# A graph network kernel: six gathers in flight, indices a block ahead, ACT's order changed, source tables split in place

## The reference

```python
edge_in = concatenate([edges, nodes[receivers], nodes[senders]], axis=-1)
h = relu(edge_in @ We1 + be1)
new_edges = h @ We2 + be2
agg = segment_sum(new_edges, receivers, num_segments=nodes.shape[0])
```

## Time and profile before

| | us |
|---|---|
| runs, median of 3 | 4964.16 |
| lowest and highest run | 4954.04, 4967.15 |
| the profiled execution | 4958.28 |
| its span | 4956.7 |
| PE busy | 4118.4 (83%) |
| VectorE busy | 3063.9 (62%) |
| POOL busy | 2552.3 (51%) |
| ACT busy | 1450.4 (29%) |

### The profile page before, as it was taken

How to read it: one execution, slowest core, us unless ns; L and a number is a source line. 1 busy time by engine, 2 the same in 40 slices (tenths; PEclk the granted TensorE clock), 3 DMA queues, 4 the chain that set the end, 5 groups by cost and what they waited for, 6 DMA issues and landing times.

```text
span 4956.7 us, 144137 instructions
## 1 busy us (share of the span) xinstructions
PE 4118.4 (83%) x56332; PEld 3710.4 (75%) x56332; DVE 3063.9 (62%) x4215; ACT 1450.4 (29%) x2353; POOL 2552.3 (51%) x2291
## 2 busy tenths in 40 slices
PE   1777799987999981999999999899758989999596
PEld 0566688887999981777777777777548988888596
DVE  5999888881111023777777777777437777777612
ACT  0333599990000012222222222222222222222100
POOL 0388766665665676666666666666003433333200
PEclk9766899998999995999999999999859999999798
DMA  5510488889999955776676777677326766666496
GB/s 173 203 30 29 144 317 321 323 320 315 397 383 417 417 199 187 226 232 220 227 235 228 227 235 229 224 230 236 128 78 219 235 207 205 221 221 214 135 399 260
DMA packets 430602, 1170.77 MB, mean 236 GB/s; under 512 B 111223, under 2 KB 250470, under 8 KB 422760
## 3 DMA queue, kind: packets, MB, share of 16 engines
q1 hardware_dynamic: 331910, 929.09, 53.0%
q0 software_dynamic: 66016, 114.12, 7.9%
q10 hardware_dynamic: 32256, 121.34, 6.2%
HBM read 798.21 MB, written 368.14 MB: 235 GB/s over the span
## 4 chain that ended last, share of the span: by engine, by line
DMA 41%; issue 27%; POOL 16%; PE 9%; DVE 4%; POOLq 2%; SPq 1%; ACT 0%; ACTq 0%; DVEq 0%
DMA feat_slot<-SK,sidx_p 18%; DMA arena<-tab_l_src,SK 17%; POOL arena L843 6%; POOL feat_slot L920 5%; POOL arena L967 4%; PE PS L1254 4%; DMA sidx_p<-SK 2%; DMA SK<-in_src_dram 2%; PE PS L1422 1%; PE PS L1023 1%; PE PS L1426 0%; SPq L460 0%; POOLq L890 0%; SPq L461 0%; PE PS L1442 0%
## 5 line engine op out<-in xcount | busy, mean ns | idle before, releaser
L920 POOL DMA_INDIRECT feat_slot<-SK,sidx_p x900 | 1114.1, 1238 | 568.7 <-DMA feat_slot<-SK,sidx_p 294.7
L967 POOL DMA_INDIRECT arena<-tab_l_src,SK x864 | 976.5, 1130 | 525.0 <-DMA arena<-tab_l_src,SK 241.8
L843 POOL TENSOR_TENSOR arena<-arena 128x448 f32<-128x448 f32 x343 | 365.6, 1066 | 808.6 <-DVE arena L2287 808.6
L1422 PE MATMUL PS<-arena 128*128 128x128 bf16 x7203 | 651.8, 221 | 124.5 <-DVE arena L2330 64.9
L1254 PE MATMUL PS<-arena 128*128 128x192 bf16 (+1 forms) x7203 | 615.4, 248 | 107.5 <-DVE arena L2130 61.9
L1254 PEld LDWEIGHTS PS<-arena 128*128 128x128 bf16 x7203 | 607.0, 98 | 114.4 <-DVE arena L2130 62.2
L1426 PE MATMUL PS<-arena 128*128 (+1 forms) x7203 | 610.4, 194 | 0.0
L1353 PE MATMUL PS<-arena 128*128 (+1 forms) x6267 | 591.4, 223 | 0.0
L1422 PEld LDWEIGHTS PS<-arena 128*128 128x128 bf16 x7203 | 457.4, 99 | 148.0 <-issue 138.0
L1426 PEld LDWEIGHTS PS<-arena 128*128 128x128 bf16 x7203 | 446.0, 99 | 1.1
L1353 PEld LDWEIGHTS PS<-arena 128*128 128x128 bf16 x6267 | 427.8, 100 | 3.8
(11 more groups left out here) (254 smaller groups left out, 6957.0 us busy)
## 6 DMA issues: line engine op xcount, KB each, us to landing
arena<-slot_rows SPq DMA_DIRECT2D x343, 448.0 KB
arena<-cnt_t SPq DMA_DIRECT2D x147, 896.0 KB
hots<-arena ACTq DMA_DIRECT2D x175, 672.0 KB
arena<-hots SPq DMA_DIRECT2D x175, 672.0 KB
arena<-cnt_t SPq DMA_DIRECT2D x147, 672.0 KB
cnt_t<-arena SPq DMA_DIRECT2D x49, 1568.0 KB
cnt_s<-arena SPq DMA_DIRECT2D x49, 1568.0 KB
arena<-cnt_s SPq DMA_DIRECT2D x49, 896.0 KB
```

The source lines that it names most:

```text
L843: pool.tensor_tensor(hid3[i][:, 2 * n:3 * n], hid3[i][:, n:2 * n], upper3[i][:, n:2 * n], ALU.subtract)\
L920: pool.indirect_dma_start(feat_slot, bass.IndirectOffsetOnAxis(ap=sidx_p[odd][:, n:n + 1].bitcast(u32), axis=0), fwin[h][:, t * D:(t + 1) ...
L967: pool.indirect_dma_start(qgot[n % 3][:, slot_of[t] * P:(slot_of[t] + 1) * P], None, tab_src[4], bass.IndirectOffsetOnAxis(ap=gidx[odd][:, ...
L1422: last = nc.tensor.matmul(PS[:, to:to + P], selS[c][:, cut], qsplit[:, (b * 3 + s) * H:(b * 3 + s + 1) * H], start=s == 0, stop=False, ski ...
```

## The change

- A gather waits for the sixth one back: six semaphores `q_in`, one per tile of a chunk. The add waits for the six of its chunk.
- The index fetch of a pair is issued after the second chunk of the pair before. The first one is issued ahead of the waits for the tables.
- ACT handles the relu of a gathered place one place later, behind `keep_features` of q (that is, of place q-3), and before the store and relu of the slot place q-2.
- VectorE does residual and last part of a gathered place one place later too, ahead of `select_rows` of q.
- The source table is split straight from `NV`, first, as soon as the linear has left it (remainder in `qrest`); `dtab` second. SP waits for the target table's store alone; in pass 4 it stores the source table behind the load of `dtab`, for the gathers; in pass 5 the source table is neither stored nor loaded.

The diff, without what belongs to the general passes, which don't run here:

```diff
@@ -122 @@
 NW = carve(51, NB * H).rearrange("p (b f) -> p b f", b=NB)
-NV = carve(76, NB * H).rearrange("p (b f) -> p b f", b=NB)
+NV = carve(75.5, NB * H).rearrange("p (b f) -> p b f", b=NB)
 TB = carve(101, NB * (D + 1))
@@ -249 @@
 dsplit = carve(36.75, NB * 3 * H, bf16)
-dtab = carve(73.5, NB * H)
-qtab = carve(98, NB * H)
+qrest = carve(100, NB * H)
+dtab = carve(124.5, NB * H)
 hots_c = [carve(73.5 + 5.25 * c, HOTS, bf16) for c in range(NC)]
@@ -369 @@
 splits_lo = sem("splits_lo")
-tabs_in = [sem(f"tabs_in{i}") for i in range(2)]
+dtab_in = sem("dtab_in")
+src_stored = sem("src_stored")
 slot_in = [sem(f"slot_in{c}") for c in range(NC)]
@@ -406 @@
 gate_out = sem("gate_out")
+q_in = added[4:7] + [gate_in, gate_out, ft_in]
@@ -433 @@
 SOURCES = [1, 3, 6]
-TAB_STORES = [16, 32, 48, 64, 32, 64, 80]
+TAB_STORES = [16, 32, 48, 64, 16, 32, 48]
 ON_V = (2, 5)
@@ -536 @@
         eng.wait_ge(signal, j * SEQ + ((2 * last if kind == "slots" else 2 * last + 1) + 1 - SEQ))
-
-def gathers_landed(eng, j, tiles):
-
-    for i in range(LIVE):
-        if tiles > i:
-            eng.wait_ge(feat_put[i], j * (PUTS * 16) + (NS * PUTS * 16 + (tiles - i + LIVE - 1) // LIVE * 16))
@@ -643 @@
         sp.dma_start(dtab[:, 0:NB * w_].rearrange("p (b f) -> p b f", b=NB), tab[k].rearrange("(b p) f -> p b f", p=P))\
-            .then_inc(tabs_in[0], 16)
-        sp.dma_start(qtab, nodes(tab_src[k])).then_inc(tabs_in[1], 16)
+            .then_inc(dtab_in, 16)
+        if k == 4:
+            sp.dma_start(nodes(tab_src[4]), NV[:, :, :].rearrange("p b f -> p (b f)")).then_inc(src_stored, 16)
+            sp.wait_ge(src_stored, 16)
         sp.wait_ge(splits_lo, 2 * NC * (m + 1))
@@ -765 @@
             sp.dma_start(nodes(tab[4]), NW[:, :, :].rearrange("p b f -> p (b f)")).then_inc(tab_stored, 16)
-            sp.dma_start(nodes(tab_src[4]), NV[:, :, :].rearrange("p b f -> p (b f)")).then_inc(tab_stored, 16)
         elif k == 5:
             sp.dma_start(tab[5].rearrange("(p b) f -> p b f", p=P), NW[:, :, 0:D]).then_inc(tab_stored, 16)
-            sp.dma_start(nodes(tab_src[5]), NV[:, :, :].rearrange("p b f -> p (b f)")).then_inc(tab_stored, 16)
         else:
@@ -942 @@
-        pool.wait_ge(tab_stored, TAB_STORES[4])
-        pool.wait_ge(splits_lo, 2 * NC)
-
-        def body(j, odd, first=False):
+        def fetch_sources(j, odd):
             start = pool.value_load(start_i[0:1, bass.ds(j + NS, 1)], min_val=0, max_val=E - WE)
-            if not isinstance(j, int) or j >= 2:
-                for i in range(LIVE):
-                    pool.wait_ge(feat_put[i], j * (PUTS * 16) + (NS - 1) * (PUTS * 16))
             pool.dma_start(gidx[odd][:, :], src[bass.ds(start, WE)].rearrange("(p t) -> p t", p=P)).then_inc(gidx_in, 16)
+
+        def body(j, odd, first=False, more=True):
             for n in range(NCH):
@@ -961 @@
                     tile = n * TN + t
-                    i = tile % LIVE
-                    pool.wait_ge(feat_put[i], j * (PUTS * 16) + (NS * PUTS * 16 + tile // LIVE * 16))
-                    pool.nop(nofuse=True)
+                    if not first or n > 0:
+                        pool.wait_ge(q_in[t], j * (NCH * 16) + n * 16)
+                        pool.nop(nofuse=True)
                     pool.indirect_dma_start(qgot[n % 3][:, slot_of[t] * P:(slot_of[t] + 1) * P], None, tab_src[4],
                                             bass.IndirectOffsetOnAxis(ap=gidx[odd][:, tile:tile + 1].bitcast(u32), axis=0))\
-                        .then_inc(feat_put[i], 16)
+                        .then_inc(q_in[t], 16)
+                if n == 1 and more:
+                    fetch_sources(j + 1, 1 - odd)
+
+        fetch_sources(0, 0)
+        pool.wait_ge(src_stored, 16)
+        pool.wait_ge(splits_lo, 2 * NC)
         body(0, 0, first=True)
         body(1, 1)
-        with pool.Fori(1, PAIRS_N // 2) as i:
+        with pool.Fori(1, PAIRS_N // 2 - 1) as i:
             body(i * 2, 0)
             body(i * 2 + 1, 1)
+        body(PAIRS_N - 2, 0)
+        body(PAIRS_N - 1, 1, more=False)
@@ -1685 @@
         hid_, upper_ = (hid, upper) if k == 4 else (hid3, upper3)
-        for i, (tb, sp_, wd) in enumerate(((dtab, dsplit, w_), (qtab, qsplit, H))):
-            act.wait_ge(tabs_in[i], 16 * (m + 1))
+        act.wait_ge(lin_kept_q, UNITS["l1pq"] * (m + 1))
+        for i, (tb, sp_, wd, rest) in enumerate(((NV.rearrange("p b f -> p (b f)"), qsplit, H, qrest), (dtab, dsplit, w_, dtab))):
+            if i == 1:
+                act.wait_ge(dtab_in, 16 * (m + 1))
             t3 = tb[:, 0:NB * wd].rearrange("p (b f) -> p b f", b=NB)
+            r3 = rest[:, 0:NB * wd].rearrange("p (b f) -> p b f", b=NB)
             s3 = sp_[:, 0:NB * 3 * wd].rearrange("p (b s f) -> p b s f", b=NB, s=3)
...
                 act.wait_ge(splits_res, c + (1 + NC * (2 * m + i)))
-                nc.scalar.activation(s3[:, bass.ds(c * CH, CH), 1, :], t3[:, bass.ds(c * CH, CH), :], ACT.Copy)\
+                nc.scalar.activation(s3[:, bass.ds(c * CH, CH), 1, :], r3[:, bass.ds(c * CH, CH), :], ACT.Copy)\
                     .then_inc(splits_mid, 1)
@@ -1733 @@
-        def messages(j, odd, q):
+        def messages(j, odd, q, only):
...
             i = (q + odd) % 2
+            if kind != only:
+                return
             if kind == "slots":
@@ -1757 @@
                 keep_features(j, odd, q)
+                if q >= 3 or not first:
+                    messages(*earlier(j, odd, q, 3), "natural")
                 if q >= 2 or not first:
                     store_hots(*earlier(j, odd, q, 2))
-                    messages(*earlier(j, odd, q, 2))
+                    messages(*earlier(j, odd, q, 2), "slots")
         pairs(act, body)
...
             store_hots(PAIRS_N, 0, q)
-            messages(PAIRS_N, 0, q)
+            messages(PAIRS_N, 0, q, "slots")
         for i in range(4):
@@ -2242 @@
         hid_, upper_ = (hid, upper) if k == 4 else (hid3, upper3)
-        for i, (tb, sp_, wd) in enumerate(((dtab, dsplit, w_), (qtab, qsplit, H))):
+        for i, (tb, sp_, wd, rest) in enumerate(((NV.rearrange("p b f -> p (b f)"), qsplit, H, qrest), (dtab, dsplit, w_, dtab))):
             t3 = tb[:, 0:NB * wd].rearrange("p (b f) -> p b f", b=NB)
+            r3 = rest[:, 0:NB * wd].rearrange("p (b f) -> p b f", b=NB)
             s3 = sp_[:, 0:NB * 3 * wd].rearrange("p (b s f) -> p b s f", b=NB, s=3)
...
                 dve.wait_ge(splits_hi, c + (1 + NC * (2 * m + i)))
-                V.tensor_tensor(t3[:, at, :], t3[:, at, :], s3[:, at, 0, :], ALU.subtract).then_inc(splits_res, 1)
+                V.tensor_tensor(r3[:, at, :], t3[:, at, :], s3[:, at, 0, :], ALU.subtract).then_inc(splits_res, 1)
             with dve.Fori(0, NC) as c:
...
                 dve.wait_ge(splits_mid, c + (1 + NC * (2 * m + i)))
-                V.tensor_tensor(s3[:, at, 2, :], t3[:, at, :], s3[:, at, 1, :], ALU.subtract).then_inc(splits_lo, 1)
+                V.tensor_tensor(s3[:, at, 2, :], r3[:, at, :], s3[:, at, 1, :], ALU.subtract).then_inc(splits_lo, 1)
@@ -2376 @@
                 dve.wait_ge(agg_made, count_at(j, q) - 2)
-            gathers_landed(dve, j, (c + 1) * TN)
+            for t in range(TN):
+                dve.wait_ge(q_in[t], j * (NCH * 16) + (c + 1) * 16)
             n = TN * H // 2
@@ -2421 @@
                 old = None if first and q < 2 else earlier(j, odd, q, 2)
+                older = None if first and q < 3 else earlier(j, odd, q, 3)
                 if old:
                     add_sources(*old)
+                if older and place(older[0], older[2])[0] == "natural":
+                    residual(*older)
+                    last_part(*older)
                 select_rows(j, q)
...
                 select_sums(j, q)
-                if old and place(old[0], old[2])[0] == "natural":
-                    residual(*old)
-                if old:
+                if old and place(old[0], old[2])[0] == "slots":
                     last_part(*old)
```

More of the change, by code:

```diff
@@ L737, in general @@
                 sp.wait_ge(tab_stored_g if k < 4 else tab_stored, TAB_STORES[k])
+                if k in (4, 5):
+                    sp.dma_start(nodes(tab_src[k]), NV[:, :, :].rearrange("p b f -> p (b f)")).then_inc(src_stored, 16)
                 z = acc[k].rearrange("(r p) f -> p r f", p=P)
@@ L814, in general @@
                 pool.wait_ge(tab_stored_g if k < 4 else tab_stored, TAB_STORES[k])
+                if k in (4, 5):
+                    pool.wait_ge(src_stored, 16 * (k - 3))
                 idx = lambda c: bass.IndirectOffsetOnAxis(ap=gcol[:, c:c + 1].bitcast(u32), axis=0)
```

## The result

| | before | after |
|---|---|---|
| runs, median of 3 (us) | 4964.16 | 4880.48 |
| lowest and highest | 4954.04, 4967.15 | 4871.77, 4882.65 |
| the profiled execution, its span | 4958.28, 4956.7 | 4871.77, 4870.2 |

The ratio is 0.9844 with a 95% interval of 0.9816 to 0.9872. The forecast of 4887 lies 7 us off the median.

What follows compares the result with a forecast made beforehand. POOL's gathers and its waits were taken as first cause of 63.3 us a pair, TensorE nearly the bound. Gains of 43 (pair loop) + 11 (pass 4 start) + 23 (pass 5 start) = 77 us gave 4887 us, range 4800 to 4935.

Steps and rivals of the forecast that it cites:

- The pair loop: Pass 4's 24 pairs: a pair falls from 63.3 to 61.5 us, 43 us in all.
- POOL's waits for landings: Pair loop: POOL's waits for earlier gathers to land, 6.7 us a pair, nearly go with six in flight.
- The ring: Pair loop: slot meet, ACT copy and relu, VectorE steps, next meet; 9.19 us against TensorE's 8.50, five times a pair.
- The turn of the loop: Pair loop: TensorE's issue stall and slower clock once per two pairs, 3.9 us a turn, 1.8 a pair.
- row numbers: Pair loop: POOL's wait for fetched indices, 3.2 us a pair, goes with the earlier index fetch.
- SP and the hot store: Pair loop: selection-matrix store issued 0.84 us later, costed at nothing; up to 5.9 us a pair if cover is gone.
- rival (1): Pair loop: the order's chain doesn't bind; 58.0 us a pair, 161 us off, 4803 us; chance 0.17.
- Pass 4: Start of the pair loop: 8 us from POOL's puts plus 3 from ACT's copy, 11 us gained, bounds -3 and 21.
- Pass 5: Its start: splits begin sooner behind the linear, 23 us gained, bounds 14 and 25.
- (2): Pair loop: gathers stay late because of other traffic; pair stays 63.3 us, 34 us off, 4930 us; chance 0.17.
- (3): Pair loop: repeated TensorE stalls lower its granted clock; 69.0 us a pair, 5067 us; chance 0.06.
- (4): Pair loop: POOL becomes the bound, every gather 1.70 us beside denser VectorE; 72.9 us a pair, 5160 us; chance 0.03.

Runs made afterwards that it cites:

- e7: Kernel before with six gathers in flight, index fetch left where it was: 4862.14 us, ratio 0.9826.
- e1: Changed kernel with ACT's and VectorE's order in the pair loop put back as before: 4833.21 us, ratio 0.9740.
- e4: Kernel before with the new order of ACT and VectorE alone: 4938.17 us, ratio 0.9958.
- e9: Changed kernel, new order kept, with ACT's store of the selection matrices one slot place earlier: 4851.09 us, ratio 0.9781.
- e5: e1 with ACT's store of the selection matrices one slot place earlier: 4742.28 us, ratio 0.9592.
- e8: Kernel before with the early index fetch alone, four gathers in flight: 4877.39 us, ratio 0.9853.
- e3: Kernel before with POOL's part alone, six gathers in flight and the early index fetch: 4861.45 us, ratio 0.9799.
- e2: Changed kernel with VectorE doing both selects ahead of the gathered place's residual and last part, ACT's new order kept: 4841.57 us, ratio 0.9750.
- e6: Kernel before with the tables' part alone (source table split from NV, not loaded): 4922.25 us, ratio 0.9932.
- e10: Kernel before with only ACT's store of the selection matrices one slot place earlier: 5027.95 us, ratio 1.0140.

## Why the prediction was right

**The pair loop.** Forecast 61.5 us, measured 62.03; forecast 43 us off the loop (1.8 a pair), measured 42.9 (1.7 a pair from the fifth on). The mechanism was right, and two sizes in it were off in opposite directions:

- POOL's waits for landings go: 234.6 to 15.6 us. That two more gathers' time covers the longest landing held (longest wait now 1.2 us, e7 1.1).
- The ring binds in five of a pair's cycles: forecast 9.19, measured 9.39, the hop to TensorE 0.24 where I estimated 0.07. That is 4.4 us a pair in place of 3.5. e1 shows it by taking it away, e4 by putting it alone on the kernel before, e9 by leaving it with everything else cleared.
- The turn of the loop was priced at 1.8 us a pair and is less. In e5, where hardly anything else is late, a pair takes 57.31 against 56.2, so 1.1 at most. That made up for most of what the ring cost more, which was luck.

**Two of its terms were right in sum and not in parts.** I took 6.7 us (landings) and 3.2 us (row numbers) off POOL's pair as if both were needed. e7 and e8 show that either is enough to reach some 60.2 from the fifth pair on, below the ring's 62.0. Beside six in flight the early fetch is worth 0.27% or nothing (e3 against e7, with intervals that overlap).

**SP and the hot store at nothing.** In the changed kernel that is nearly so: TensorE waits 22.0 us for slot features from 2000 to 3500, and e9 puts the whole of it, with the last block, at 31 us. But I argued it from the 3.2 us of the earlier trace rows, and that row is one of a loop in which other waits gave the features their time. In e1, e2 and e3, without the ring, the same loads are the next bound. So rival (1), 58.0 a pair and 4803, could not have come from the orders alone: e1 is 4833. It took the store too, and then it was 4742.

**The starts.** Pass 4: forecast 11, measured 14.8, of which 2 were there before the tables. One pair of executions says little here: the first fetch comes at 1947.4 to 1952.9 us in the six kernels with the tables' part and at 1953.0 to 1975.1 in the six without, and the means are 11 us apart. Pass 5: forecast 23, measured 21.7. e6 measured both together at 34. The median came out 7 us below the forecast, no more than the 8.5 us by which the unchanged rest of the program differed between the two profiled executions.

**The rivals.** (2) falls with POOL's 15.6 us. (3) falls with the clock: 0.99 in the loop against 0.97, and round one of the ring's stalls (columns as in the earlier trace rows) it was at its upper level of 2.4 GHz:

```profile
2334.00:2337.00 3.00, 2.39 (x37) 2.15 (x36) 3.00 (x5) 0.00 (x0) 1.56 (x2) 1.00 1.05 316
```

(4) falls with a gather's mean of 1.131 us, the same as in the earlier trace rows. Its 1.70 against 1.13 set a put beside a gather. Like beside like, from 2000 to 3300 us in the kernel before, a gather takes 0.95 us in the median while VectorE is idle and 1.23 while VectorE runs `TENSOR_TENSOR` on SBUF operands alone: the slowing is there, and much smaller than (4) took it.

What the prediction didn't ask is the question that was worth most: whether a part of the change costs something that the rest doesn't need. The ring was in the sum, as a term of 5 x 0.7; priced against a version without the order it would have said to leave the order out.

## What to carry to other kernels

When a change has parts that cure the same wait in two ways, price each with the other already in: here the new order was worth 21 us alone and cost 47 beside the deeper gathers. A wait that costs nothing in one profile costs nothing only as long as that profile's bound stands. List what comes second before you call a load hidden: the store moved one place earlier was worth 73 to 91 us once the gathers and the ring were out of the way, and cost 67 us while the gathers were the bound.

## What the runs showed of the hardware

- The hop from VectorE's select to TensorE's waiting matmul was 0.24 us in the loop. In the pairs written out ahead of it (the code has two of them outside the hardware loop), in the same execution, it was 0.05 (select_sums from 2027.68 for 0.62 us, meet at 2028.35), and the cycle 9.21. In the loop the waits compare with a value out of a register; that this is the cause was not tried.

```profile
2027.68 0.62 DVE L2342 TENSOR_TENSOR arena<-sd,iota 128x896 bf16<-128x896 bf16 x1
```
```profile
2028.35 0.34 PE L1352 MATMUL PS<-arena 128*128 128x128 bf16 x3 [0.42 <-DVE arena L2342]
```

- From 2000 to 3300 us the changed kernel had 96 stalls of TensorE at `select_sums`, 63.9 us in all and 0.8 the longest, with a granted clock of 1.00. In the same stretch e1, with fewer stalls of up to 4.0 us, had 0.99, and the kernel before 0.98.
- A gather's landing is not a fixed time. With four in flight, the fourth behind could start 5.85 us after a gather's end in the median, and 6.45 with the store one place earlier. That the store's own traffic is the reason is likely from the transfers under e10, and not shown by a run.
